# Attention scores of a macaron block on Trainium2: from six bf16 products on 103 rows to fp32 products on four groups of 32 rows

## What is computed

```python
x = x + 0.5 * ffn(layernorm(x))      # router, top 6 of 64 experts, plus a shared expert
x = x + attn(layernorm(x))
x = x + 0.5 * ffn(layernorm(x))

def attn(x):                         # 16 heads of 16 values, T = 512
    q = rope(x @ wq)
    lat = x @ w_down                 # 256 -> 128
    k, v = rope(lat @ wk_up), lat @ wv_up
    scores = q . k / 4, masked: a token sees the pages of 64 tokens up to its own
    return softmax(scores) @ v @ wo
```

## Time and profile before

| what | value |
|---|---|
| median of 3 runs | 2078.44 us (2070.83 to 2088.26) |
| the profiled execution, its own time | 2082.85 us |
| its span, first to last instruction | 2081.1 us |
| mean granted TensorE clock over the span | 0.951 of full speed |
| attention stage | about 560 to 1432 us |
| one full turn (11 of them, 768.3 to 1303.6 us) | 48.66 us |

### The profile page before, as it was taken

One profiled execution on the slowest core, in us unless ns is written; L12 is line 12 of the kernel. 1 busy time (PEld: TensorE's weight loads), 2 busy tenths in 40 slices (PEclk: granted clock), 3 DMA queues, 4 the chain that ended last, 5 costly groups with the idle time before them and its releaser, 6 DMA issues. The chain is left out here.

```text
span 2081.1 us, 33794 instructions
## 1 busy us (share of the span) xinstructions
PE 1787.1 (86%) x11330; PEld 1141.7 (55%) x11330; DVE 1253.2 (60%) x3079; ACT 1071.1 (51%) x2132; POOL 871.6 (42%) x938
## 2 busy tenths in 40 slices
PE   5999997999737899999999999996999999866773
PEld 3656655888622344445545444553556656755672
DVE  4878885443345677777777777761878877322221
ACT  4766763111024577777777777773667765100000
POOL 1101101688736566666666665500101100555553
PEclk9999998999967899999999999997999999999986
DMA  2443533999734333434444444312233431777763
GB/s 82 129 129 128 161 130 107 254 260 260 154 102 122 112 113 114 113 113 113 121 125 130 131 119 113 95 41 83 79 92 105 130 114 53 202 189 183 179 164 40
DMA packets 218233, 269.71 MB, mean 130 GB/s; under 512 B 18378, under 2 KB 185322, under 8 KB 218094
## 3 DMA queue, kind: packets, MB, share of 16 engines
q1 hardware_dynamic: 193518, 230.20, 36.6%
q0 software_dynamic: 24576, 37.77, 9.8%
HBM read 136.17 MB, written 80.25 MB: 104 GB/s over the span
## 5 line engine op out<-in xcount | busy, mean ns | idle before, releaser
L1259 DVE TENSOR_REDUCE a_smax<-a_p_ring 128x1 f32<-128x512 f32 (+2 forms) x768 | 353.8, 505 | 153.6 <-PE a_p_ring L1346 148.5
L1161 ACT ACTIVATE a_probs<-a_p_ring 128x512 f32<-128x512 f32 x640 | 363.8, 606 | 104.1 <-PE a_p_ring L1358 102.4
L1346 PE MATMUL a_p_ring<-p_ks,p_qs 100*128 100x512 bf16 (+3 forms) x1024 | 247.4, 306 | 45.9 <-ACT a_probs L1161 20.6
L611 ACT ACTIVATE e_silu<-e_p_up 88x256 f32<-88x256 f32 x128 | 48.6, 380 | 458.7 <-PE e_p_up L653 360.8
L653 PE MATMUL e_p_up<-e_xT,h_w 128*88 128x128 f32 x2048 | 259.1, 282 | 0.0
L47 POOL TENSOR_TENSOR f_rstd<-f_mv,eps 128x4 f32<-128x4 f32 x32 | 25.6, 799 | 554.2 <-DVE f_mv L41 549.6
L1358 PE MATMUL a_p_ring<-p_qs,p_ks 103*128 103x512 bf16 (+3 forms) x1024 | 244.2, 305 | 7.0 <-ACT a_probs L1161 6.7
L653 PEld LDWEIGHTS e_p_up<-e_xT,h_w 128*88 128x88 f32 x2048 | 243.3, 164 | 0.2
L455 PE MATMUL f_p_up<-f_xnT,f_ws1T 128*128 128x512 f32 x384 | 187.7, 612 | 1.5 <-ACT f_xnT L250 1.5
L575 POOL DMA_INDIRECT e_got<-rows,slot_token x128 | 126.5, 988 | 145.0 <-issue 135.3
L625 DVE TENSOR_TENSOR e_hidden<-e_silu,e_p_up 88x256 f32<-88x256 f32 x128 | 53.4, 417 | 221.5 <-ACT e_silu L611 165.3
(11 more groups left out here) (142 smaller groups left out, 3243.4 us busy)
## 6 DMA issues: line engine op xcount, KB each, us to landing
h_w<-w_in SPq DMA_DIRECT2D x128, 352.0 KB
p_qs<-a_parts SPq DMA_DIRECT2D x192, 128.0 KB, 2.5
p_ks<-a_parts SPq DMA_DIRECT2D x192, 128.0 KB, 2.5
h_w<-w_in SPq DMA_DIRECT2D x128, 176.0 KB
rows<-f_row SPq DMA_DIRECT2D x32, 640.0 KB, 6.9
h_x<-x_in SPq DMA_DIRECT2D x16, 512.0 KB, 5.9
acc<-h_x SPq DMA_DIRECT2D x16, 512.0 KB, 2.8
acc<-blank SPq DMA_DIRECT2D x16, 512.0 KB, 4.0
```

Source lines behind the costliest of these rows:

```text
L1161: nc.scalar.activation(to[:], p_score[s][:], ACT.Exp, scale=SCALE).then_inc(score_free[s], 1)
L1259: ins = nc.vector.tensor_reduce(smax[:, t, 4 * g + h:4 * g + h + 1], p_score[s][:, at:at + length], AX.X, ALU.max)
L1346: ins = nc.tensor.matmul(p_score[s][:, at:at + length], qs[1 - u][0:SR + MASK, 4 * g + h, t * P:(t + 1) * P], ks[1 - u][0:SR + MASK, 4 * g ...
```

## The change

Scores are computed in fp32 itself. Four heads lie on four groups of 32 rows of the array: 16 rows of values, 4 of the mask, one of the maximum. `qs` and `ks` hold fp32, one tile of [128, 4, 512] for each of three buffers (`BUFFERS`) in place of two. Heads (h, quad) are dealt so that one weight layout serves it. The steps `S1` and `S2` become one step `SS`, a burst that takes four banks of the ring at once, one for each row group: in full turns two banks are of the first pass of one quad (heads 0, 1) and two are of the second pass (heads 2, 3), and in the burst after it the other way round. TensorE waits for all four banks before the first of its matmuls; the four tiles of a piece are issued one after another. `HIGH`, `SPLIT` and `NEG` are gone, with the parts, the casts and POOL's subtractions; a STACK is 4 transfers from `qk` (16 a batch in place of 24), and the maxima need one transfer instead of three. `MAX` becomes four fp32 matmuls of `smax` (8 columns) against the identity, and the minus sign lies in the row of -1 in `ks`. A burst's banks are reduced by DVE and exponentiated by ACT as before, with the same instructions on the same sizes. The order of a pass is A, C, B of the first quad, then A, B of the second (C serves both), and the fractions of the placed steps are new.

The diff, cut to its core:

```diff
-Q_SLOTS = [HIGH, HIGH, MIDDLE, HIGH, LOW, MIDDLE]
-K_SLOTS = [HIGH, MIDDLE, HIGH, LOW, HIGH, MIDDLE]
+GROUP = 4
+ROWS = HD + MASK
+RING_BANKS, OUT_BANKS, BUFFERS = 6, 2, 3
+ORDER = [("A", 0), ("C", 0), ("B", 0), ("A", 1), ("B", 1)]
+def bursts(maxima, probs, group, second):
+    if probs is None:
+        return [("SS", maxima + (group, second, (0, 1, 2, 3)), None)]
+    if maxima is None:
+        return [("SS", None, (probs, group, second, (0, 1, 2, 3)))]
+    return [("SS", maxima + (group, second, (0, 1)), (probs, group, second, (2, 3))),
+            ("SS", maxima + (group, second, (2, 3)), (probs, group, second, (0, 1)))]
...
+MAXIMA = [(0.56, ("MAX", 0))]
+LATE_MAXIMA = [(0.08, ("MAX", 1))]
+SHARE = {"SS": 4, "PV": 1, "OUT": 1}
...
-    pre.qs = [sb(f"qs{u}", [P, H, T], BF16) for u in range(2)]
-    pre.ks = [sb(f"ks{u}", [P, H, T], BF16) for u in range(2)]
+    pre.qs = [sb(f"qs{u}", [P, QUADS, T]) for u in range(BUFFERS)]
+    pre.ks = [sb(f"ks{u}", [P, QUADS, T]) for u in range(BUFFERS)]
...
+        def take_banks(step, scores):
+            of_maxima, of_probs = [], []
+            for n in range(GROUP):
+                if step[2] is None or (step[1] is not None and n % 2 == 0):
+                    of_maxima.append(scores.next())
+                else:
+                    of_probs.append(scores.next())
...
+                    for h in range(GROUP):
+                        sp.dma_start(to[group_rows(h, 0, HD), 2 * e:2 * e + 2, :],
+                                     qk[r][group_rows(h, 0, HP), :]).then_inc(stack_loaded[e], 16)
...
-                        elif step[0] == "NEG":
-                            nc.gpsimd.tensor_scalar(rest[:], half, -1.0, None, ALU.mult)
...
-                        elif step[0] == "HIGH":
-                            nc.gpsimd.tensor_tensor(qk[r][:], qk[r][:], parts[r][:, HIGH, :],
...
-                            nc.scalar.copy(parts[r][:, HIGH, :], qk[r][:]).then_inc(high_ready, 1)
...
+                            for _, s, used, _, _, _, _, _ in tiles:
+                                wait_count(pe, score_free[s], used)
+                            for q, block, at, length in score_pieces(group):
+                                for h, s, used, which, queries, keys, rows, quad in tiles:
+                                    of = group_rows(h, 0, rows)
+                                    if which == "maxima":
+                                        ins = nc.tensor.matmul(p_score[s][:, at:at + length],
+                                                               queries[of, quad + q, block * P:(block + 1) * P],
+                                                               keys[of, quad + q, 0:length], start=True, stop=True)
...
+                                    if at + length == T:
+                                        ins.then_inc(score_ready[s], 1)
...
                             for t in range(NT):
-                                ins = nc.tensor.transpose(p_misc[m][:, t * P // 2:(t + 1) * P // 2].bitcast(BF16),
-                                                          smax_parts[e][:, t, :], ident16[:])
+                                ins = nc.tensor.matmul(p_misc[m][0:H // 2, t * P:(t + 1) * P],
+                                                       smax[:, t, e * H // 2:(e + 1) * H // 2], w.ident[:],
+                                                       start=True, stop=True)
```

More of the change, by code:

```diff
@@ new lines, in passes @@
+def passes(maxima, probs, entering=False):
+    steps = []
+    for group, second in ORDER:
+        steps += bursts(maxima, probs, group, second)
+        if probs is None:
+            continue
+        if (group, second) == ("A", 0) and entering:
+            steps += [("PV", probs - 1, "B", 1)]
+        elif (group, second) == ("C", 0):
+            steps += [("PV", probs, "A", 0)] + [("OUT", 2 * probs - 1)] * entering
+        elif (group, second) == ("B", 0):
+            steps += [("PV", probs, "C", 0)]
+        elif (group, second) == ("A", 1):
+            steps += [("PV", probs, "B", 0)]
+        elif (group, second) == ("B", 1):
+            steps += [("PV", probs, "A", 1), ("PV", probs, "C", 1), ("OUT", 2 * probs)]
+    return steps
@@ L769, in place @@
     return steps_of(spread + list(placed))
-def with_stacks(steps):
-    out = list(steps)
-    for half in range(2):
-        at = max(out.index(("S2", 2 * half + 1, "C", GROUP_BANKS["C"] - 1)), out.index(("SPLIT", K_TILES[half])))
-        out.insert(at + 1, ("STACK", half))
-    return out
-ENTERING = PROJECT + NEXT_INPUT
-FULL_TURN = with_stacks(place(OUTPUTS, VALUES + TAIL + ENTERING + MAXIMA + LATE_MAXIMA))
 def of_batch(b, steps):
@@ L818, in with_stack @@
-def with_stack(half, steps):
-    out = list(steps)
-    at = max(out.index(("S2", 2 * half + 1, "C", GROUP_BANKS["C"] - 1)), out.index(("SPLIT", K_TILES[half])))
-    return out[:at + 1] + [("STACK", half)] + out[at + 1:]
-SECOND_SCORES = place(quads_probs(2, QUADS), VALUES + ENTERING + MAXIMA + [(0.06, ("OUT", 1))])
-SECOND_SCORES = with_stack(1, SECOND_SCORES)
-SECOND_SCORES.insert(SECOND_SCORES.index(("SPLIT", K_TILES[0])) + 1, ("STACK", 0))
+    from_to(0.0, 0.34, of_batch(0, passes((0, 0), None)))
@@ L828 @@
+SECOND_SCORES = place(passes((1, 0), None) + passes((1, 1), 1) + [("PV", 1, "B", 1)],
+                      VALUES + ENTERING + [(-0.01, ("MAX", 1)), (0.45, ("MAX", 0))])
 TURNS = ([(b, [step]) for b, step in FIRST_INPUT + FIRST_SCORES]
@@ L875, in open_attention, with group_rows @@
     return pre
[L878 to L880 removed]
+def group_rows(h, first, last):
+    return slice(HP * h + first, HP * h + last)
 def load_attention(sp, w, dram, pre):
@@ L1218, in _ @@
             def _(dve):
-                swap_pairs = [i ^ 8 for i in range(32)]
+                swap_pairs = [i ^ 2 for i in range(32)]
                 def statistics(n, t):
@@ new lines, in turn @@
+                        if kind == "SS":
+                            of_maxima = take_banks(step, scores)[0]
+                            if not of_maxima:
+                                continue
+                            _, e, group, second, heads = step[1]
+                            if (group, second, heads[0]) == ("A", 0, 0) and e in turned:
+                                dve.wait_ge(*turned[e])
+                            for h, (s, used) in of_maxima:
+                                at_head = e * H // 2 + 2 * h + second
+                                dve.wait_ge(score_ready[s], used + 1)
+                                if group == "C":
+                                    ins = nc.vector.tensor_reduce(
+                                        smax[:, 1, at_head:at_head + 2],
+                                        p_score[s][:].rearrange("p (q t) -> p q t", q=2), AX.X, ALU.max)
+                                else:
+                                    for _, t, at, length in score_pieces(group):
+                                        ins = nc.vector.tensor_reduce(smax[:, t, at_head:at_head + 1],
+                                                                      p_score[s][:, at:at + length], AX.X, ALU.max)
+                                ins.then_inc(score_free[s], 1)
+                        elif kind == "MAX":
+                            turned[step[1]] = misc_ready[m], use + 1
```

397 lines of the change are left out of this document (131 added, 266 removed).

## The result

| | before | after |
|---|---|---|
| median of the runs | 2078.61 us (2070.83 to 2088.26) | 2334.66 us (2330.85 to 2339.65) |
| the profiled span | 2081.1 us | 2337.9 us |
| mean granted TensorE clock | 0.951 | 0.918 |

The changed kernel takes 1.1231 times as long (95% interval 1.1179 to 1.1283). The direction was right and the size was not: +119 us were forecast, +256 came, and 2334.66 us lies above the range of 2150 to 2245.

A forecast was written before the change was run, and what follows sets the result against it. TensorE was taken as the bound. Full turns +116 us, last turns +7, clock +11 and start -15 gave +119 on the profiled 2082.85, 2202 us; with the median 4.4 lower, 2198 us was forecast, its own range 2150 to 2245.

The forecast's parts named there:

- score matmuls: Full turn: 80 banks at 0.22 us (17.6) become 20 bursts at 0.87 us (17.4), so -0.2 us.
- `MAX`: Full turn: four bf16 transposes in 0.22 us become four fp32 matmuls in 0.87 us, twice a turn, +1.3 us.
- waits: TensorE's idle in a full turn: 9.8 us, of which 7.0 in seven pairs and 2.0 more behind `NORM`; before, 2.46.
- What bounds the kernel: Full turns: TensorE is the bound by a margin of a quarter; relieving ACT, POOL and queues counts only in the start.
- Waits inside the pairs: Two bursts with nothing between: the second idles 0.95 us, or 1.03 in group B, for banks; 7.0 us a turn.
- Changes of tiling: Full turn: switches between row-group bursts and other TensorE steps cost 0.5 us, bounds 0 and 1.8.
- The clock: Full turns: one fall to 1.2 GHz costing 1.7 us, in half of the 13 turns, +11 us.
- The rival that had the clock swing: Second half of full turns: short idles in every pair make the clock oscillate, +4 us a turn, 2245 us; chance 0.14.
- The start: Before the first full turn: waits for stacked parts and split maxima shrink, -15 us of 19.1, bounds -19 and +10.
- The last turns: Turn 14, without projections, keeps the pairs' waits: +7 us; turn 15, paced by ACT: 0.

The follow-up runs named there:

- small matmuls: Changed kernel with three small fp32 matmuls (9 behind `NORM`) into a free bank inside the waits of second bursts with nothing before them: 2283.72 us, ratio 1.0948.
- `NORM` late: Changed kernel with `NORM` moved from fraction 0.87 of the turn to 0.985, behind the turn's last exponentials: 2320.75 us, ratio 1.1137.

## Why the prediction was right in its sign and wrong in its size

Two steps of the prediction's sum failed in the turns: what a burst costs with its changes of tiling, and how often the clock falls. A third failed in the start. One full turn, term by term; +8.9 and the clock's +0.85 were forecast, +15.8 us came:

| term | forecast | measured | from |
|---|---|---|---|
| score matmuls and changes of tiling | -0.2 +0.5 | +3.8 | 20 x 1.07 against 17.6 |
| `MAX` | +1.3 | +1.5 | 0.97 against 0.22, twice |
| waits | 9.8 less 2.46 | 8.2 less 2.46 = +5.7 | waits of PE |
| clock | +0.85 | +3.4 to +4.1 | small matmuls; the two turns of `NORM` late |
| not placed | | +0.6 to +1.3 | difference |

Some 0.5 us of what isn't placed is in the bare pairs: TensorE counts as busy for 1.13 to 1.15 us with a burst that has a wait behind it (2.02 less 0.87), not for 1.07.

**What bounds the kernel: right.** TensorE did; ACT and POOL were relieved by 3 and 11 us a turn for nothing.

**Waits inside the pairs: right,** and the main term of the right sign. 0.95 and 1.03 were forecast, 0.87, 0.99 and 0.84 stand in one turn, and putting work into the pairs took the waits from 8.2 to 3.9. From start to start of a bare pair 1.82 and 1.90 were forecast and 1.99 to 2.14 measured: the wait is shorter because the burst ahead of it is longer. Behind `NORM` 3.0 were forecast and 2.10 measured here, 1.2 to 2.8 in the nine turns. One reading was missing: with the wait for all four banks it isn't only the ring's size that counts but that one late bank holds four tiles. A wait for each tile's own bank was worth 2.1 us a turn alone, 1.1 of it at the same clock, and 2.3 once the pairs were filled, 1.4 of it at the same clock.

**Changes of tiling: this step failed.** "Bounds 0 and 1.8; I take 0.5." The count of 16 changes a turn was about right, their price wasn't. I read it from PV at 0.09 to 0.13 us a change, and then let it vanish wherever a wait was near, and took 0.87 for the burst from PV's 1.00 less that change. A burst costs 0.86 + 0.2 to the next step: 3.5 us a turn more than forecast, 46 us in 13 turns. The warning was in my own row: PV took 1.00 us to the next step and not 0.87, with its change of tiling, and there are 20 bursts. The Trainium skill (TensorE: Matmul & The Clock Gate, "Measured speedup vs the span model") would have made it 1.12 us by an estimate from its 3.07x, and I set it aside. The trace stands near it: 1.07 was measured, 3.2 times as fast as one after another. Issued back to back, though, the second set took 0.86, four times as fast.

**The clock: this step failed too.** "I take it in half of the 13 turns, +11." It fell in every turn, for some 10 us on average and not 3.4, and cost 3.4 to 4.1: 33 to 42 us too little in 13 turns. The rival that had the clock swing, with 0.14, was the right one in kind, and its +4 us a turn beyond the 0.85 was somewhat too large. Against it I had put that full turns with a wait of 1.4 us never fell. That was one wait in a turn otherwise full; the changed turn has nine idles, most of 0.66 to 0.99 us, with TensorE busy 6.7 of 8.7 us ahead of the first fall. The Trainium skill (TensorE: Matmul & The Clock Gate, "A second HAM failure mode: psum-queue depth-cycling") tells of a kernel in which frequent short idles between groups of matmuls, from cycling through banks, made the clock swing between its two levels. The trace agrees: nine idles a turn, and a mean clock of 0.92.

**The start: this step failed, sign included.** -15 was forecast, +22.8 came. 11.1 of it is the expert stage, some 10 for the 18 added mask transfers: I had counted transfers in attention only ("12 of the 30") and none of those ahead of it. Between that stage and the first `V` it is 4.0 us less. The rest lies in the two stretches behind, which took 110.0 us and now take 125.7. The wait for stacked parts did fall, from 13.0 to 5.2 us, and the maxima's wait of 6.1 went, but 12.8 us of waits for DVE's reductions (4.0 before) took much of their place, so TensorE's idle fell by 4.3 us only, from 30.6 to 26.3. Its busy time rose by 20, from 79.4 to 99.4, at a mean clock of 0.70 (0.79 before). That is the same two terms again, bursts and clock, which I hadn't priced in the start at all; how they share the 20 us isn't separated. With the small matmuls in the waits the two stretches took 117.1 us, so some 8 us of it are the clock's.

**The last turns:** +18.1 for +7 in turn 14. Its waits are 10.2 us, where 7 were forecast and the profile before shows none; the rest are its 20 bursts, which I hadn't priced there, its `MAX` steps and a clock of 0.94.

Added up: 82 us of the missing 138 lie in the 13 turns (46 for the bursts and 33 to 42 for the clock, less 21 for waits forecast too long, the rest small or not placed), 38 in the start, 18 in the last turns and behind. That waits were forecast too long hid part of the two errors. The text named what would prove it wrong: "PE longer busy in the score groups than 17.4 us a turn, which would put the price in the array". That came true with 21.4, beside the waits and not in their place, and what it puts in the array is the way in and out of the tiling.

Not tried: two buffers in place of three. With the order of the changed kernel the second buffer would be written while TensorE still reads it, and it would have needed other places for its steps.

## What to carry to other kernels

A burst that takes four of six buffers at once turns a pipeline into lock step: before making a unit of work larger, count what is left of the ring (a short step put between takes a buffer too), and let each part wait for its own buffer. Price a changed mode by start to next start with its surroundings in it, and multiply by how often it is entered. When TensorE gets many short idles, add the clock to their price: a turn with the same work and the same waits took 59.2 us or 67.6.

## What the runs showed of the hardware that I had not expected

- Four fp32 tiles on four row groups run fully side by side once under way (0.86 us a set of 512 columns), and 0.2 us is paid for each way in and out.
- Useless matmuls in the waits made the kernel 51 us faster, by the clock (mean 1.00 in the turns in place of 0.92).
- Eighteen more small transfers (24 of 32 and 40 KB in place of six of 48 and 64 KB) ahead of a stage in which the DMA engines are busy 0.96 of the time made it some 10 us longer, although the issue of most takes 0.3 to 0.6 us. The next transfers left 3.7 us later than before, and with sixteen of the masks moved away, which gave the 10 us back, still 2.9 us later.
- A tile can wait for its bank while tiles on other row groups work, and the profile then shows no idle time of TensorE: busy 486.90 of 486.90 us is not a full array.
